# Rotary parts spread over the expert slots, earlier maximum products, and the maximum added once in four key blocks

## The reference

```
xn = (x - mean) / sqrt(var + 1e-5)                     # x: [2, 1024, 256]
Q, K, V = xn @ W_q, xn @ W_k, xn @ W_v                 # 16 query heads, 4 key heads, 16 dims per head
Q, K = rope(Q), rope(K)                                # rotate pairs (x0, x1) by the position's angle
w = softmax(Q K^T / 4)                                 # 4 query heads share a key head
attn = (w V) @ W_o
for e in range(8):                                     # top 2 of 8 experts per token
    ffn += ((clip(silu(xn @ Wg[e]), -7, 7) * (xn @ Wu[e])) @ Wd[e]) * w_e
out = x + attn + ffn
```

## Time and profile before

| | |
|---|---|
| median of 3 runs | 576.74 us (575.99 to 579.41) |
| profiled execution | 576.07 us, of which 574.3 us is the span |
| TensorE busy | 526.5 us (92%), 3464 matmuls |
| VectorE, ScalarE, GpSimd busy | 396.3, 383.5, 173.2 us |
| mean granted TensorE clock | 0.976 of full |
| slot 0's silu to slot 38's | 61.60 to 226.32 us |

### The profile page before, as it was taken

One profiled execution on the slowest core, in us unless ns is written; L12 is line 12 of the kernel. 1 busy time (PEld: TensorE's weight loads), 2 busy tenths in 40 slices (PEclk: granted clock), 3 DMA queues, 4 the chain that ended last, 5 costly groups with the idle time before them and its releaser, 6 DMA issues.

```text
span 574.3 us, 9921 instructions
## 1 busy us (share of the span) xinstructions
PE 526.5 (92%) x3464; PEld 249.3 (43%) x3464; DVE 396.3 (69%) x920; ACT 383.5 (67%) x548; POOL 173.2 (30%) x208
## 2 busy tenths in 40 slices
PE   1996748897999998999999999999999999999997
PEld 1832324454555554444444444444444444444433
DVE  4578756961666666587788887888888788785123
ACT  3421412431333433799999999999999999998673
POOL 3015854541222210012416422551344342600000
PEclk9997987897999999999999999999999999999999
DMA  8950235566642120310511421422224113100101
GB/s 293 375 184 1 80 133 170 169 183 193 170 138 74 59 62 29 103 38 19 131 47 45 115 58 41 102 65 75 57 58 119 31 57 84 30 2 21 46 29 55
DMA packets 39566, 53.72 MB, mean 94 GB/s; under 512 B 7936, under 2 KB 25728, under 8 KB 39520
## 3 DMA queue, kind: packets, MB, share of 16 engines
q1 hardware_dynamic: 32624, 40.25, 23.9%
q0 software_dynamic: 3408, 9.31, 5.9%
q10 hardware_dynamic: 3488, 3.55, 1.8%
HBM read 36.18 MB, written 16.65 MB: 92 GB/s over the span
## 4 chain that ended last, share of the span: by engine, by line
PE 73%; DVE 12%; DMA 6%; issue 3%; ACT 2%; SPq 2%; POOL 2%; DVEq 0%; ACTq 0%; POOLq 0%
PE bank L1249 21%; PE bank L1239 9%; PE bank L1112 9%; PE bank L1167 8%; PE bank L1129 7%; PE bank L1235 6%; PE bank L1184 4%; PE bank L1285 3%; DMA k_st<-rope_low 3%; PE bank L1122 2%; DMA rows_out<-xn 2%; DVE xn_t L907 2%; DVE xn L983 2%; SPq L378 1%; PE bank L1072 1%
## 5 line engine op out<-in xcount | busy, mean ns | idle before, releaser
L702 ACT ACTIVATE big<-bank 128x1024 f32<-128x1024 f32 x256 | 252.9, 1024 | 18.6 <-PE bank L1239 18.3
L1249 PE MATMUL bank<-big,v_st 128*32 128x256 f32 (+1 forms) x1472 | 148.3, 474 | 2.8 <-DVE xn L983 2.8
L1239 PE MATMUL bank<-qs,kb 64*128 64x512 f32 x512 | 120.0, 408 | 0.7 <-ACT big L702 0.7
L904 DVE TENSOR_REDUCE mx<-bank 128x1 f32<-128x512 f32 x128 | 87.8, 686 | 27.9 <-PE bank L1129 20.1
L899 DVE TENSOR_REDUCE mx<-bank 128x1 f32<-128x512 f32 x128 | 87.9, 687 | 22.1 <-PE bank L1114 20.0
L1167 PE MATMUL bank<-big,xn 128*128 x156 | 82.6, 654 | 15.9 <-ACT xn L671 15.4
L907 DVE CUSTOM_DVE_ANT_0 xn_t<-bank,xn_t 128x512 f32<-128x512 f32 x128 | 87.5, 684 | 4.5 <-PE bank L1129 1.5
L657 ACT ACTIVATE xn_t<-bank 128x512 f32<-128x512 f32 x128 | 76.7, 599 | 20.4 <-PE bank L1114 12.2
L1239 PEld LDWEIGHTS bank<-qs,kb 64*128 64x128 f32 x512 | 57.7, 185 | 19.4 <-ACT big L702 12.3
L1112 PE MATMUL bank<-ka,qs 64*128 64x512 f32 x128 | 63.4, 495 | 0.4 <-DVE mx L904 0.4
L1114 PE MATMUL bank<-ka,qs 64*128 64x512 f32 x128 | 63.3, 495 | 0.0
(11 more groups left out here) (140 smaller groups left out, 611.7 us busy)
## 6 DMA issues: line engine op xcount, KB each, us to landing
qs<-q_hl SPq DMA_DIRECT2D x64, 128.0 KB, 2.7
rows_out<-xn SPq DMA_DIRECT2D x39, 128.0 KB, 2.6
ka<-k_st SPq DMA_DIRECT2D x16, 256.0 KB
kb<-k_st SPq DMA_DIRECT2D x16, 256.0 KB
xs<-in_L_attn_x SPq DMA_DIRECT2D x4, 512.0 KB, 6.3
big<-in_L_ffn_Wg SPq DMA_DIRECT2D x16, 128.0 KB, 6.5
big<-in_L_ffn_Wu SPq DMA_DIRECT2D x16, 128.0 KB, 6.6
big<-in_L_ffn_Wd SPq DMA_DIRECT2D x16, 128.0 KB, 6.5
```

The lines of the kernel that those rows point to most:

```text
L702: act.activation(probs[kt % 2][:, 2 * j:2 * j + 2, :].rearrange("p r q -> p (r q)"), st_ps[j][:, :], ACT.Exp, scale=1.0 / math.sqrt(HD)).t ...
L904: nc.vector.reduce_max(mx[h][:, STEPS + k, 1:2], max_bank(v, i), axis=X_AXIS).then_inc(mx_taken, 1)
L1239: last = mm(out[i], kb[p][half[i], kt // QT, keys], qs[q][half[i], j, :], start=False, stop=True, skip_group_check=kt % 2 == 1)
L1249: last = mm(o_ps[32 * r:32 * (r + 1), columns], v_st[p][:, key_block(kt), :], probs[kt % 2][:, r, columns], start=(kt == 0 and columns.sta ...
```

## The change

1. Rotation parts go to slots 0, 2, 4, 6, 8, 10, 12, 16, 20, 24, 28, 32 in place of 0 to 11. Keys and queries are loaded as soon as the parts that they need are stored (slots 6, 10, 11, 14, 15, 21 ...).
2. ScalarE copies the projections of block 3 too, before slot 0, which frees their banks, and the maximum products are spread over the last 26 slots (13 to 38) in place of 21. `copy_projected(3)` stands between `high_part(0)` and the first slot. Of block 3 and of the query parts, parts 9 and 11 have their cosine on VectorE as parts 3, 5 and 7 do; part 10 goes to GpSimd.
3. The maximum is added once in four key blocks. For this a key part has a second set of differences: K[0:256] - K[256:512] and then K[256:512] - K[128:384], written to partitions 64 to 127. A key part's store becomes 8 DMAs of 64 rows x 512 in place of 4 of 64 rows x 768; its rounding and low half work on 128 partitions x 512 in place of 64 x 768. In attention, steps kt = 1 and 5 of a unit become even steps like 0, 2, 4 and 6; kt = 3 and 7 stay odd.

```diff
-    k_st = nc.dram_tensor("k_st", [B, KV, STACK, 2, KCOLS], F32, kind="Internal").ap()
+    k_st = nc.dram_tensor("k_st", [B, KV, STACK, 2, 2 * HALF], F32, kind="Internal").ap()
...
+        PART_SLOTS = (0, 2, 4, 6, 8, 10, 12, 16, 20, 24, 28, 32)
+        KEYS_LOAD, FIRST_LOAD, SECOND_LOAD, LATE_LOAD = 6, 10, 14, 20
...
-            return sum(32 if PARTS[o][1] < 2 else 64 for o in range(q % 3, q, 3))
-        SHARED = 21
+            return sum(32 if PARTS[o][1] < 2 else 128 for o in range(q % 3, q, 3))
+        def stored_up_to(q, n):
+            return sum(32 if PARTS[o][1] < 2 else 128 for o in range(n, q + 1, 3))
+        SHARED = 26
...
-            return kt // QT * QT + 2 * (1 - kt % 2) + kt // 2 % 2
+            return kt // QT * QT + (3, 1, 2, 0)[kt % QT]
...
                     for j, half in enumerate((rope_hi, rope_hi, rope_lo, rope_lo)):
-                        sp.dma_start(k_st[b, :, HD * j:HD * (j + 1), k % 2, :],
-                                     half[n][0:KV * HD, :].bitcast(F32)).then_inc(done, 16)
+                        for u in range(2):
+                            sp.dma_start(k_st[b, :, HD * j:HD * (j + 1), k % 2, u * HALF:(u + 1) * HALF],
+                                         half[n][KV * HD * u:KV * HD * (u + 1), :].bitcast(F32)).then_inc(done, 16)
...
+            for t in range(SLOTS + 2):
+                q = part_at(t)
+                if q is not None:
+                    store_part(q)
+                if t == KEYS_LOAD:
+                    parts_stored(1)
+                    load_ka(0, 0)
+                if t == FIRST_LOAD:
+                    parts_stored(4)
+                    load_q(0, 0, 0, [0])
...
+                if t == SECOND_LOAD:
+                    parts_stored(6)
+                    load_q(0, 1, 1, [0])
...
+                if t >= 2:
+                    store_y(t - 2, (t - 2) % 4)
...
+            copy_projected(BLOCKS - 1)
+            for t in range(SLOTS):
+                expert(t, t % 2, first=t == 0, last=t == SLOTS - 1, beside=shared_with(t))
+                if part_at(t) is not None and part_at(t) + AHEAD - 1 < NP:
+                    high_part(part_at(t) + AHEAD - 1)
...
-                        nc.vector.tensor_tensor(rope_a[n][0:rows_q, HALF:KCOLS], rope_a[n][0:rows_q, 0:QUART],
-                                                rope_a[n][0:rows_q, QUART:HALF], ALU.subtract).then_inc(rope_done, 1)
+                        nc.vector.tensor_tensor(rope_a[n][rows_q:P, 0:QUART], rope_a[n][0:rows_q, 0:QUART],
+                                                rope_a[n][0:rows_q, QUART:HALF], ALU.subtract)
+                        nc.vector.tensor_tensor(rope_a[n][rows_q:P, QUART:HALF], rope_a[n][0:rows_q, QUART:HALF],
+                                                rope_a[n][0:rows_q, P:P + QUART], ALU.subtract).then_inc(rope_done, 1)
...
-                if kt % 2 == 0:
+                if kt % QT == 0:
                     for i in parts:
                         mm(out[i], ones_r[half[i], :], ms[v][half[i], j, :], start=True, stop=False)
...
-                        if kt % 2 == 0 and not last:
+                        if kt % QT < QT - 1 and not last:
                             scores(2 * p + h, h, p, kt + 1, s + 1, 0)
                             values_between(2 * p + h, h, p, kt, s, u, (u + 2, ahead, 1 - p, kt))
```

More of the change, by code:

```diff
@@ L430, in _ @@
                     load_m(0)
[L431 to L442, removed]
+                if t >= 2:
+                    store_y(t - 2, (t - 2) % 4)
+            for m in range(3):
+                sp.wait_ge(qk_stored[m], stored_before(NP + m))
             def period(g, p, last):
@@ L545, in _ @@
                 gather_rows(t)
-                q = t - 4 + AHEAD
-                if q < NP:
+                if part_at(t - 4) is not None and part_at(t - 4) + AHEAD < NP:
+                    q = part_at(t - 4) + AHEAD
                     if q >= 3:
@@ L636, in _, with copy_projected @@
             act.activation(gate_t[:, 1, :], gate_t[:, 0, :], ACT.Exp).then_inc(gate_exp, 1)
-            for k in range(BLOCKS - 1):
+            def copy_projected(k):
                 act.wait_ge(pj_ready, 3 * (k + 1))
@@ L641, in _ @@
                     act.activation(projected(k, m)[0:rows_m, :], pj_ps[k][m][0:rows_m, :], ACT.Copy).then_inc(pj_copied, 1)
+            for k in range(BLOCKS - 1):
+                copy_projected(k)
             act.wait_ge(hot_tile_ready, 1)
@@ L958, in take_y @@
                 nc.vector.tensor_copy(y_s[q], y_ps[i] if y is None else y).then_inc(y_copied, 1)
[L960 to L963, removed]
-                rope_sum(t + AHEAD)
-                rope_step(t + AHEAD)
-            for t in range(NP, SLOTS):
+            for t in range(SLOTS):
                 todo = shared_with(t)
@@ L972, in _ @@
                     first_max(n)
-                take_y(t - 2, (t - 2) % 4, t % 2, 16 * ((t - 2) // 4))
+                if t >= 2:
+                    take_y(t - 2, (t - 2) % 4, t % 2, 16 * ((t - 2) // 4) if t >= 6 else None)
+                if part_at(t) is not None:
+                    rope_sum(part_at(t) + AHEAD)
+                    rope_step(part_at(t) + AHEAD)
             for t in range(SLOTS - 2, SLOTS):
@@ L1212, in _ @@
             to_columns(0, 0)
-            for t in range(NP):
-                expert(t, t % 4, 16 * ((t + 1) // 4 + 1), first=t == 0)
-            pe.wait_ge(stacks_padded, 5)
-            for t in range(NP, SLOTS):
+            for t in range(SLOTS):
                 if t == SLOTS - SHARED:
+                    pe.wait_ge(stacks_padded, 5)
+                    pe.wait_ge(pj_copied, 3 * BLOCKS)
                     pe.wait_ge(ka_loaded[0], 32)
-                expert(t, t % 4, 16 * ((t + 1) // 4 + 1), last=t == SLOTS - 1, beside=shared_with(t))
+                expert(t, t % 4, 16 * ((t + 1) // 4 + 1), first=t == 0, last=t == SLOTS - 1, beside=shared_with(t))
             act_columns(SLOTS - 1, (SLOTS - 1) % 4)
@@ L1238, in scores @@
                         pe.wait_ge(mx_taken, banks)
-                    last = mm(out[i], kb[p][half[i], kt // QT, keys], qs[q][half[i], j, :], start=False, stop=True, skip_group_check=kt % 2 == 1)
+                    last = mm(out[i], kb[p][half[i], kt // QT, keys], qs[q][half[i], j, :], start=False, stop=True, skip_group_check=kt % QT > 0)
                 if parts[-1] == 1:
```

71 lines of the change are left out of this document (33 added, 38 removed).

## The result

The changed kernel takes 580.6 us (median of 16 runs, 578.02 to 584.36) against 575.84 us for the kernel before (16 runs): a ratio of 1.0084, with a 95% interval of 1.0063 to 1.0104. Forecast were 562.5 and a range of 552 to 572. It is slower, and the range missed it by 8.6 us.

What follows compares the result with a forecast made beforehand. TensorE was taken to bound slots 18 to 38, key-store DMAs to stall the early slots. From 576.07 us, 8.6 (slots), 3.3 (attention) and 1.8 (last group) came off: 562.4, stated as 562.5, range 552 to 572.

Steps and rivals of the forecast that it cites:

- Key stores: Slots 0 to 8: larger key parts at an unchanged store rate bound these slots; key part 2 lands at 103.0 us.
- a rival: Key stores don't bound: eight DMAs spread better or overlap, slots 0 to 8 run at 3.0 us; 548 us, chance 0.12.
- Loads before slot 13: Query load issued about 110 us, items start at 117: covered by 4 us or so, no cost counted.
- its signs of being wrong: Slot 8 done before 95; VectorE waits over 2 us in slots 16 to 32; even step at 2.6; slot 13 awaiting queries.
- rival D: The experts win nothing: stalls only move, by an undervalued port, clock or load wait; 571 us or so, chance 0.17.
- Parts beside items: Slots 16 to 32 with a part and items: TensorE waits 0.8 us each, 4 in all; slot 32's key stores add 1.
- rival C: VectorE, held by GpSimd products, falls behind in slots with a part and items: 24.5 us lost, 582 us, chance 0.08.
- Attention: 14 units with maxima ahead: two steps each fall from 2.61 to 2.47 us, 3.9 us in all, 3.3 taken.
- an even step that ScalarE stretches to 2.6: Sign against the forecast in attention, where an even step was to take 2.47 us.
- Last group: Attention without maxima ahead: four places lose a 0.46 us ones product each, 1.8 us gained.
- Start of slot 0: Three ScalarE copies ahead of the table load start slot 0 1.5 us later, at 63.1 us.

Runs made afterwards that it cites:

- key_only: The kernel before with only the new key differences, 8 DMAs per key part, ones once in four blocks and values split in three steps of four: 592.57 us, ratio 1.0279.
- slot15: The changed kernel with the maximum items spread over the last 24 slots (from 15) in place of 26: 573.62 us, ratio 0.9946 to the kernel before.
- before_wide: The kernel before with the key scratch laid out in 64 rows per half, 768 columns kept and no spreading: 568.15 us, ratio 0.9871.
- split_even: The changed kernel with values split only where kt is even, ones product still once in four blocks: 574.83 us, ratio 0.9960 to the kernel before.

## Why the prediction was wrong

*Key stores* ("if the stores keep their rate ... key part 2 lands at 103.0"). The mechanism was right, down to `high_part(5)` in slot 8 and the y stores queued behind; the term was mis-sized. The first part lands 17.3 us after its first issue in place of 14.9, and the next two 11.3 and 12.5 us apart in place of 11.3 and 10.4: key part 2 is there at 109.4, not at 103.0, and 2.0 of these 6.4 us are the later start. The last part came at some 82 GB/s in place of 95. From slot 0's silu to slot 12's it took 56.0 us in place of 50.9: 5.1 of the error. The larger fault was in what I made of it. I had the rule of the Trainium skill that names the shape as the cause (the section that the prediction cites) and let it decide only between 103.0 and a rival; that the third part would land 10 us later than before (103.0 for 92.76) was in my own figures. `key_only`, where slots 0 to 38 take 12.8 us more, shows what that costs.

*Loads before slot 13* ("covered by 4 us or so; if it were not, slot 13 would start later by the difference"). This step failed. The load's second half was issued at 122.46, not 110, landed 6 us later, not 3, and the half clock came on top: 8.1 us for a term that I had put at nothing. I set a load at 110 against a slot 13 at 117. But in SyncE's order the load stands behind the store of part 5, which is ready only in slot 10 (118.01 here), and its second half behind one more y store: both ends move together, and slot 10's own start of 107.4 left hardly any cover. `slot15` gives 7.0 of it back. The prediction had this wait among its signs of being wrong, and among the stalls of rival D.

*Parts beside items*: 4 + 1 us forecast, and 2.9 measured from slot 12 to slot 38 (109.7 - 98.7 - 8.1). Right in kind and nearly in size: behind the parts of slots 16 and 24 TensorE waits 1.0 and 1.1 us for a maximum on VectorE. That 580.6 lies next to the 582 of rival C is chance. Rival C had the wrong mechanism for the loss, though VectorE held by GpSimd is real where the parts stand slot by slot (`before_wide`).

*Attention* ("a step falls from 2.61 to 2.47: 3.9 us ... I take 3.3"). This step failed and changed sign: 3.8 us more than 340.0, with the last group's gain inside. The steps at kt = 1 and 5 went from 2.61 to 2.65, not to 2.47, and those at kt = 2 and 6 from 2.47 to 2.63, where I had seen no change. A run of the chain over TensorE was read as TensorE being the bound. ScalarE's second exponential, the split step's first halves, and the next second exponential form a loop of 2.64 us; a whole step in between let it catch up, and in a row it sets the step. I had added up ScalarE's own time (2.4 to 2.5) but not the loop through both engines, though "an even step that ScalarE stretches to 2.6" was among the signs of being wrong. `split_even` gives 5.3 us back, and only by ending the runs. The ones products in these units were worth 0, because behind them stands a second loop of 2.61 us, through the maximum's copy.

*Last group*: 1.8 forecast, 1.5 to 1.8 measured. *Start of slot 0*: 1.5 forecast, 1.1 in the profiles.

The sum closes by stretches of the two profiles, 582.5 against the 562.4 forecast: 11.1 us more from slot 0 to slot 38 (5.1 stores, 8.1 at slot 13, 2.1 less beside items), 7.2 more behind slot 38 (2.1 longer in place of 5.1 shorter; against the 340.0 of the other kernels it would be 8.9), and 2.0 of a later slot 0, most of it the start that moves by itself.

## What to carry to other kernels

When a chain of waits shows one engine nearly all the way, look one row further at the other engine's wait: if two engines release each other within a step, add up the way around. Work taken off beside that loop is worth nothing, and only a shorter way around helps. This spread-out schedule was held by its slowest stream: size the DMAs by the rate that their own shape had in the trace, and change the shape before moving them. A wait that a load covers has to be placed with both ends moved by the change, since a load that depends on the same slots moves along with its user.

## What the runs showed that I had not expected

One layout of a 1 MB scratch, 4 against 64 as the slowest dimension of a store, was worth 13.4 us here and 7.2 on the kernel before (768 KB a part), though it put more key loads in front of the query load. SyncE's issue of the eight DMAs fell with it, from 12.4 to 4.9 us in the second part: a slow store also holds its issuing engine. Spreading and quick stores gain 7.5 and 7.2 us apart, and with the split and the pause mended 25 together. And a clip of 0.27 us takes 1.35 beside a GpSimd product, five times its own length.
